# Attention scores: a lead of 20 units in place of 31, then four units a period in place of three

## The reference, cut to what matters

```python
H = 16
hd = C // H                       # 16 channels a head
q = _l2norm(q) * sm
k = _l2norm(k)
scores = jnp.einsum('bhqd,bhkd->bhqk', q, k)
probs = jax.nn.softmax(scores, axis=-1)
o = jnp.einsum('bhqk,bhkd->bhqd', probs, v)
```

## Time and profile before

| | us |
|---|---|
| median of 3 runs | 3171.84 (3170.88 to 3175.58) |
| profiled execution, its time | 3174.25 |
| profiled execution, its span | 3172.5 |
| PE busy | 3097.2 (98%) |
| DVE busy | 2759.5 (87%) |
| ACT busy | 2703.8 (85%) |
| POOL busy | 2484.2 (78%) |

### The profile page before, as it was taken

The page is one execution under the profiler, slowest core; times in us unless marked ns, Lnnn a source line. Parts: engine busy times, 40 slices in busy tenths (PEclk is TensorE's granted clock), DMA queues, the critical chain, the costliest instruction groups (busy, mean ns, idle before and its releaser), DMA issues.

```text
span 3172.5 us, 59515 instructions
## 1 busy us (share of the span) xinstructions
PE 3097.2 (98%) x23304; PEld 2631.1 (83%) x23304; DVE 2759.5 (87%) x3049; ACT 2703.8 (85%) x4496; POOL 2484.2 (78%) x638
## 2 busy tenths in 40 slices
PE   8999999999999999999999999999999999999999
PEld 6998899884699889988479988998848998888965
DVE  3999999977499999997659999999666999999963
ACT  3999999974699999995579999999558999999845
POOL 2999999971199999996139999999415999999910
PEclk9999999999999999999999999999999999999999
DMA  5222222210222232221022232223102223222100
GB/s 185 80 84 67 85 73 84 74 56 29 74 69 82 74 92 68 82 85 65 1 84 67 82 87 79 74 82 89 46 14 80 81 76 89 69 74 82 57 14 8
DMA packets 195240, 225.69 MB, mean 71 GB/s; under 512 B 77449, under 2 KB 149641, under 8 KB 193681
## 3 DMA queue, kind: packets, MB, share of 16 engines
q1 hardware_dynamic: 194960, 221.89, 22.8%
HBM read 217.37 MB, written 4.48 MB: 70 GB/s over the span
## 4 chain that ended last, share of the span: by engine, by line
PE 82%; POOL 8%; issue 4%; DVE 3%; ACT 1%; DMA 0%; SPq 0%; DVEq 0%; ACTq 0%; POOLq 0%
PE bank L1129 23%; PE bank L1109 17%; PE bank L1009 11%; PE bank L1110 10%; POOL states L674 5%; PE bank L1105 4%; PE bank L1353 4%; POOL y_gated L674 3%; PE bank L1390 2%; PE bank L1493 2%; PE bank L1378 2%; DVE states L1640 2%; PE bank L1184 1%; PE bank L1136 1%; PE bank L1281 1%
## 5 line engine op out<-in xcount | busy, mean ns | idle before, releaser
L674 POOL TENSOR_TENSOR states<-states,c_rows 128x2048 f32<-128x2048 f32 x336 | 1531.6, 4574 | 132.4 <-DVE states L1640 129.9
L1640 DVE TENSOR_TENSOR_SCAN states<-decay,bank 128x512 f32<-128x512 f32 x1376 | 1577.4, 1201 | 16.5 <-ACT decay L854 1.2
L854 ACT ACTIVATE decay<-dt,a_log 128x512 f32<-128x512 f32 x2048 | 1305.5, 710 | 0.0
L845 ACT ACTIVATE inflow_tok<-dtx_tok,b_tok 128x512 f32<-128x512 f32 x1536 | 995.7, 713 | 85.7 <-PE bank L1110 74.6
L1109 PE MATMUL bank<-ident,inflow_tok 128*128 128x128 f32 x5280 | 904.7, 280 | 35.8 <-DVE states L1640 18.7
L1129 PE MATMUL bank<-ident,states 128*128 128x128 f32 x5504 | 826.0, 273 | 6.1 <-DVE y_gated L1646 3.0
L1640 DVE TENSOR_TENSOR_SCAN y_gated<-decay,bank 128x512 f32<-128x512 f32 x672 | 777.1, 1202 | 14.0 <-ACT decay L854 5.0
L674 POOL TENSOR_TENSOR y_gated<-y_gated,c_rows 128x2048 f32<-128x2048 f32 x168 | 768.4, 4574 | 19.8 <-DVE y_gated L1640 18.1
L1109 PEld LDWEIGHTS bank<-ident,inflow_tok 128*128 128x128 f32 x5280 | 598.9, 141 | 205.7 <-issue 87.6
L1110 PE MATMUL bank<-b_diag,dtx_tok 128*128 128x128 f32 x3520 | 681.3, 275 | 0.0
L1129 PEld LDWEIGHTS bank<-ident,states 128*128 128x128 f32 x5504 | 645.0, 141 | 14.3 <-POOL states L674 7.8
(11 more groups left out here) (174 smaller groups left out, 2592.3 us busy)
## 6 DMA issues: line engine op xcount, KB each, us to landing
c_rows<-c_spill SPq DMA_DIRECT2D x256, 512.0 KB, 3.7
b_diag<-diag_ring SPq DMA_DIRECT2D x256, 128.0 KB, 2.3
xproj_w<-in_xproj_w SPq DMA_DIRECT2D x32, 320.0 KB, 3.8
in_w<-in_in_w SPq DMA_DIRECT2D x16, 512.0 KB, 4.5
out_w<-in_out_w SPq DMA_DIRECT2D x4, 1024.0 KB, 8.2
in_w<-in_fc_w SPq DMA_DIRECT2D x8, 512.0 KB, 4.3
xproj_w<-in_w SPq DMA_DIRECT2D x8, 512.0 KB, 4.7
xproj_w<-in_fc_w SPq DMA_DIRECT2D x4, 1024.0 KB, 4.7
```

Source lines behind the costliest of these rows:

```text
L674: pool.tensor_tensor(state_row, state_row, c_row.to_broadcast([P, KI, L]), ALU.mult).then_inc(weighed, PAIRS)
L845: last_tok = act.activation(inflow_tok[:, r % SLOTS, t, :], dtx_tok[:, d, t, :], ACT.Copy, scale=b_tok[:, d, t, s:s + 1])
L854: act.activation(decay[:, r % SLOTS * KI + k, :], dt[:, d, k, :], ACT.Exp, scale=a_neg[:, d, k, s:s + 1]).then_inc(decay_ready, 1)
L1640: dve.tensor_tensor_scan(state_slots[r % STATES][:, k, time], decay[:, slot, time], banks[k % INFLOW_BANKS][:, time], 0.0, ALU.mult, ALU.a ...
```

## The change

Three things. The lead has 20 units. Each of the eleven mixed periods has four units of scores (20 + 44 = 64, as 31 + 33 = 64). The first group's turn of maxima stands behind the lead, after unit 19 and no longer after unit 21. The banks and the ring of three are as they were, as are ACT's order and all work of DVE and PE in number.

```
-LEAD = 31
+LEAD = 20
...
-S_STEP = 3
+S_STEP = 4
...
-                    if u == STEPS + LEAD_BANKS - 1:
-                        pe.wait_ge(qk_t_ready, (b + 1) * (2 * NG - 1))
-                        turn_q_max(0, banks[7])
+                pe.wait_ge(qk_t_ready, (b + 1) * (2 * NG - 1))
+                turn_q_max(0, banks[7])
                 for j in range(PERIODS):
                     v, u = j * HG, LEAD + j * S_STEP
-                    if j < S_PERIODS:
+                    if j == 0:
                         scores(u)
-                        scores_t(v)
                         scores(u + 1)
-                        scores_t(v + 1)
-                        if j:
-                            scores(u + 2)
-                    else:
-                        scores_t(v)
-                        scores_t(v + 1)
-                    scores_t(v + 2)
-                    scores_t(v + 3)
-                    if j == 0:
-                        scores(u + 2)
+                    for m in range(HG):
+                        if 0 < j < S_PERIODS:
+                            scores(u + m)
+                        scores_t(v + m)
+                        if j == 0 and m < S_STEP - 2:
+                            scores(u + 2 + m)
```

## The result

The changed kernel takes 3198.72 us (median of 4 runs, 3194.72 to 3203.22), the kernel before in the same comparison 3173.71 (4 runs, 3170.88 to 3176.79). The ratio is 1.0078 with a 95% interval of 1.0060 to 1.0096: slower by 25 us. The forecast was 3195, in a range of 3181 to 3208. The profiled execution took 3202.48 us, its span is 3200.7.

What follows compares the result with a forecast made beforehand. No engine paces throughout: DVE paces the lead, PE the mixed periods, where one bank's latency decides. -21.7 + 37.4 - 0.7 + 7.7 = +22.7 us on 3171.84 gives 3195 us, range 3181 to 3208.

Steps and rivals of the forecast that it cites:

- the last turn: Turns of maxima in periods 2, 6, 10: covered by the weighing; the last one's 0.26 miss goes, 0.7 us gained.
- the low clock: PE at 1.2 GHz from about 755.8 falls on PE-paced periods 0 and 1: 7.7 us more in all (0 to 15.6).
- The mixed periods: Periods 2 to 10: fourth score waits for its period's first reduction, 2.92 becomes 3.96 us; 37.4 us more (33.5 to 43).
- The rival that DVE has room and the score is hidden: Mixed periods: added score finds its bank free, periods stay 2.92 us; 3158 us, chance 4%.
- the Trainium skill's rule on the emptying of PSUM: Mixed periods: taken as a rate, 2.4 us of reductions in 2.92 stay hidden, giving -21.7 us alone.
- this rival's turning point: Added time per mixed period below which the kernel is faster: 0.60 us; another 4% for near there and no change.
- The shorter lead: Lead and periods 0 and 1: period 2 starts 21.4 us after the first score; 21.7 us gained at full clock.
- The turn's new place costs nothing: Turn of maxima behind the lead: its copy ends near 757.1, a microsecond ahead of need; cost nothing, even at half clock.
- spread into the periods 2 to 10: Rival: half-empty lanes lower the clock in mixed periods, 36 us more if a third are hit, 3231 us; chance 6%.
- two waves: Periods 0 and 1: two bursts of units at half clock, each 0.96 us longer; 1.9 us a batch.
- a clock that swings because of small idles of PE: Skill's account of small idles between matmul groups while banks cycle; trace said to agree for the lead, at 0.50.
- The 22% for no low clock: Rival: shorter lead runs fewer units alone, so the low clock goes, taking away 7.7 us: 3187 us; chance 22%.

Runs made afterwards that it cites:

- the changed kernel at full clock: Changed kernel plus two full-height 256-column multiplications into unused bank 7 behind lead units 11, 15 and 19: 3187.92 us, ratio 1.0046 to the kernel before.

## Why the prediction came out

The time by its own sum: -21.7 for the lead, +37.4 for the periods, -0.7 for the last turn, +7.7 for the low clock, +22.7. Measured in medians: the changed kernel at full clock against the kernel before as it stood, 3187.92 - 3172.96 = +15.0, where the first three terms gave +15.0; the low clock of the changed kernel +10.8, where the fourth gave 7.7. Together that is 25.8 from two comparisons, and the direct one has 25.0. By the traces the lead at full clock gave 21.4 (4 x 21.46 against 107.2), the periods with the last turn cost 36.4, and the low clock 12.3. Of the 3.7 us between the forecast of 3195 and 3198.72, 1.9 are the starting point: the kernel before had 3173.71 in this comparison and 3171.84 in the one that the forecast was built on.

**The mixed periods: right.** 1.04 a period from 2.92 to 3.96 in the rows, and the fourth score's weights 1.90 after the start. Shorter reductions moved it by their own 0.40, another bank moved the wait to scores_t at 1.85, and without the fourth score the plain periods are 2.92 again. The rival that DVE has room and the score is hidden failed for the reason given; the Trainium skill's rule on the emptying of PSUM (TensorEngine Tiling (Array Packing), PSUM Bottleneck), taken as a rate, would have hidden it. The prediction priced this rival's turning point too high. It put it at 0.60 us of added time a period, from the 21.7 alone; with its own 0.7 and 7.7 in the sum it is 14.7 / 36 = 0.41. The measured 1.04 is beyond both. DVE is busy 25.96 of 38.57 us in these periods and still decides.

**The shorter lead: right at full clock.** Unit 20 waits for unit 19's reduction, and period 2 starts at 21.46 where 21.4 was worked out.

**The turn's new place costs nothing: right, for a reason that belongs to the short lead.** There the turn waits for unit 15, and its copy is over before unit 20 may start: the turn begins at 756.63, and the copy at 757.59 and ends at 758.19, ahead of the scores at 758.93, with the first scores_t 0.11 behind them.

```profile
756.63 0.93 PE L1360 MATMUL bank<-ident,decay 128*128 128x128 f32 x4 [0.17 <-DVE decay L1736]
757.59 0.60 ACT L925 ACTIVATE dt<-bank 128x512 f32<-128x512 f32 x1 [6.39 <-PE bank L1360]
758.93 1.22 PE L1353 MATMUL bank<-dtx_tok,dt 32*128 32x512 f32 x2 [1.37 <-DVE decay L1736]
759.04 1.23 PE L1378 MATMUL bank<-dt,dtx_tok 32*128 32x512 f32 x2
```

Behind a lead of 31 the same edit costs 6 us, which I did not foresee. The prediction did not need it.

**The low clock: right in kind, 3 us short.** The clock fell about where it was expected, lay on units that PE paces, and did not spread into the periods 2 to 10. I took 1.9 a batch, two waves. The rows have 1.8, 4.6, 2.7 and 3.2, three waves in the mean. The term counted a stretch of 3.4 to 6.8 us, although two of the four in the earlier trace rows are 10.2 long. Why the stretches grew from 30.7 to 41.0 us no run shows. The wide bounds (0 to 15.6) held it; the value inside them was a choice between two and three waves.

Two readings around it were loose. The low clock was said to hit units that DVE paces and to cost the kernel before 0.9 us a batch. It also hit the turn of maxima, behind which DVE stood idle, and cost 1.1 to 1.4 a batch by the traces of the two runs with added multiplications. And the lead was taken as agreeing with a clock that swings because of small idles of PE. The rows show the fall, to 0.50, but no such idles in PE's records ahead of it (6.08 of 6.08 us busy); that idles are the cause is not shown.

**Chances.** The 22% for no low clock was not met, but it was no idle case: with the same lead and three scores a period two of four batches had none.

## What to carry to other kernels

Before filling a free slot of an engine, count the buffers as holds: units in flight by the time from start to release, against the spacing of the bursts that take them. Here a free lane in every period was worth nothing, since a unit holds its bank for 1.9 us and the second burst comes 0.97 behind the first. And work moved from a stage paced by one engine to a stage paced by another changes what each microsecond of a slow clock costs: 30.7 us of low clock cost 4 to 6 us before the change, where DVE set the pace, and 41.0 us cost 11 to 12 after it.

## What the runs showed of the hardware that was not expected

Three full-height multiplications of 256 columns a batch, behind units 11, 15 and 19 of a stage in which DVE paces and PE works mostly one lane at a time, held the granted clock at 2.4 GHz in all four leads, where it had fallen to 1.2 for 3.4 to 10.2 us. They delayed nothing that showed: 29 reductions ran in 17.65 us without a stop, and the kernel got 4 us faster with more work in it. What PE did before the clock fell was a run of single-lane units with its matmul records busy all the time (6.08 of 6.08 us in the earlier trace rows). So a busy PE is no sign that the clock will stay.
